# An attention and mixture-of-experts block on one core: another order of the opening, and the weight maxima one step later

## What is computed

```
mod = silu(c) @ wmod                       # sa, ca, ga, sb, cb, gb for each batch
ga, gb = sign(g) * max(|g|, 0.25)
h  = layernorm(x) * (1 + ca) + sa
q, k, v = h @ qkv_w.T + qkv_b;  q, k = relu(.) + 1e-6
num = q . cumsum(k v);  den = max(q . cumsum(k), 1e-6)
x  = x + ga * ((num / den) @ out_w.T + out_b)
h  = layernorm(x) * (1 + cb) + sb
u  = rmsnorm(h @ W_in.T);  top 2 of (u @ Wr.T + bias), softmax over the two
out = sum over the two of gate * rmsnorm((silu(u Wg_e) * (u Wu_e)) @ Wd_e)
x  = x + gb * rmsnorm(out) @ W_out.T
```

## Time and profile before

| | |
|---|---|
| timed runs | 417.27, 417.74, 418.27 us |
| profiled execution | 417.46 us, of which the span is 415.5 us |
| busy share of the span | PE 85%, PEld 74%, DVE 77%, ACT 70%, POOL 59% |
| mean granted clock of PE | 0.944 of full |

### The profile page before, as it was taken

The page is one execution under the profiler, slowest core; times in us unless marked ns, Lnnn a source line. Parts: engine busy times, 40 slices in busy tenths (PEclk is TensorE's granted clock), DMA queues, the critical chain, the costliest instruction groups (busy, mean ns, idle before and its releaser), DMA issues.

```text
span 415.5 us, 12907 instructions
## 1 busy us (share of the span) xinstructions
PE 353.6 (85%) x3750; PEld 308.6 (74%) x3751; DVE 321.0 (77%) x1029; ACT 292.0 (70%) x814; POOL 245.1 (59%) x221
## 2 busy tenths in 40 slices
PE   3799999999999999984049999999999999990464
PEld 2588887888888888873039989889899999980343
DVE  4078898899999999885828878787787778780686
ACT  4344769888888888744617778778778787873595
POOL 1957566788888888865541554554545455463341
PEclk9999999999999999995559999999999999997698
DMA  7997000000000000011412323233232232213833
GB/s 237 399 361 293 4 6 21 27 29 27 25 25 25 25 25 25 28 52 36 144 38 48 66 66 69 65 69 70 57 70 64 64 71 56 65 34 101 350 98 95
DMA packets 46563, 35.68 MB, mean 86 GB/s; under 512 B 36291, under 2 KB 42070, under 8 KB 45750
## 3 DMA queue, kind: packets, MB, share of 16 engines
q1 hardware_dynamic: 41718, 21.21, 18.4%
q0 software_dynamic: 4544, 9.39, 7.0%
q10 hardware_dynamic: 272, 4.72, 3.0%
HBM read 18.69 MB, written 13.47 MB: 77 GB/s over the span
## 4 chain that ended last, share of the span: by engine, by line
PE 52%; DVE 20%; issue 9%; DMA 8%; ACT 7%; POOL 2%; DVEq 1%; SPq 0%; ACTq 0%; POOLq 0%
PE bank L1712 9%; PE bank L1713 8%; PE bank L1714 8%; PE bank L1465 5%; DVE prod L953 4%; PE bank L1727 4%; PE bank L1729 4%; PE bank L1728 4%; DMA gates_bc<-gate_rows 4%; ACT junk L846 2%; PE bank L1543 2%; DVE st L877 1%; DVE rows L1014 1%; DVE wmaxs L1049 1%; DMA dispatched<-rows,pos 1%
## 5 line engine op out<-in xcount | busy, mean ns | idle before, releaser
L570 POOL DMA_INDIRECT expert_rows<-late,to_place x78 | 81.8, 1049 | 82.9 <-DVE late L1326 70.3
L1712 PE MATMUL bank<-late,w_hi 128*128 128x256 f16 x312 | 86.3, 277 | 14.8 <-DMA late<-dispatched 13.4
L1714 PE MATMUL bank<-late,w_lo 128*128 128x256 f16 x312 | 86.2, 276 | 0.0
L1713 PE MATMUL bank<-late,w_hi 128*128 128x256 f16 x312 | 86.2, 276 | 0.0
L1312 DVE SCALAR_TENSOR_TENSOR kv<-bank,uscale,kv 128x512 f32<-128x512 f32 x78 | 58.5, 750 | 32.1 <-ACT kv L788 18.6
L547 POOL DMA_INDIRECT dispatched<-rows,pos x64 | 67.3, 1051 | 26.7 <-issue 18.4
L529 POOL TENSOR_TENSOR kv<-kv,v 128x1024 f32<-128x1024 f32 x32 | 67.6, 2134 | 16.2 <-ACT kv L691 16.2
L1465 PE MATMUL bank<-cst,kv 128*128 128x128 f32 x576 | 74.6, 281 | 1.1 <-POOL kv L529 0.9
L1465 PEld LDWEIGHTS bank<-cst,kv 128*128 128x128 f32 x576 | 69.4, 195 | 1.8 <-POOL kv L529 1.0
L788 ACT ACTIVATE kv<-bank,descale 128x512 f32<-128x512 f32 x78 | 53.6, 687 | 23.3 <-PE bank L1714 19.3
L794 ACT ACTIVATE kv<-kv 128x512 f16<-128x512 f32 x78 | 48.8, 625 | 16.9 <-DVE kv L1312 11.4
(11 more groups left out here) (231 smaller groups left out, 737.4 us busy)
## 6 DMA issues: line engine op xcount, KB each, us to landing
late<-wguT ACTq DMA_DIRECT2D x1, 4096.0 KB, 16.0
late<-expert_rows SPq DMA_DIRECT2D x1, 2064.0 KB, 11.0
gates_bc<-gate_rows SPq DMA_DIRECT2D x1, 2048.0 KB, 15.7
wd<-wdT SPq DMA_DIRECT2D x1, 2048.0 KB, 24.4
out<-kv SPq DMA_DIRECT2D x16, 128.0 KB, 1.8
late<-dispatched SPq DMA_TRANSPOSE x78
expert_rows<-late,to_place POOLq DMA_INDIRECT x78
late<-expert_rows SPq DMA_DIRECT2D x1, 1032.0 KB, 6.6
```

The lines of the kernel that those rows point to most:

```text
L570: pool.indirect_dma_start(ybuf, bass.IndirectOffsetOnAxis(ap=to_place[:, s, r:r + 1], axis=0), yt[:, s, r, :], None).then_inc(y_scat[s], 16)
L1712: mm(o, w_hi[:, w], hi, start=True, stop=False)
L1713: mm(o, w_hi[:, w], lo, start=False, stop=False)
L1714: last = mm(o, w_lo[:, w], hi, start=False, stop=True)
```

## The change

- PE runs seven bf16 matmuls (128x128 by 128x512, on a tile that POOL sets to zero) before anything else, into a bank that is used later.
- Constants have a semaphore of their own, `cst_ld`; waits that need only these name it. The output bias counts with x of batches 2 to 5.
- `wgu` is issued by SP behind `gates_bc`, not by ACT.
- The bias matmuls of batch 0 come ahead of PE's wait for hT.
- The k and v bias is split on DVE, in eight instructions, at the end of its opening; POOL's eleven go.
- The norm of batch 1: square root, reciprocal and shift are done with batch 0's, and ACT's two `xn` instructions right after hT of batch 0.
- POOL's parts of the output bias and its wait for `gates_in` come after the products of batch 1; the four gate products in steps 2 to 5, not 1 to 4. ACT's three casts for the output bias move to step 3.
- The maxima are in steps 3 to 6, and the matmuls that turn and spread them use the second third's bank, so three state matmuls go ahead of them; `weight_power` follows the first products.

```diff
+        warm = prod[:, 1, 0:2 * D].bitcast(BF16)
...
-        MAX_STEPS = range(SCALE_STEP - 5, SCALE_STEP - 1)
-        MAX_ROW = CUM[0][0:1, THIRD * P:THIRD * P + P]
-        MAX_ALL = CUM[0][:, THIRD * P:THIRD * P + 1]
+        MAX_STEPS = range(SCALE_STEP - 4, SCALE_STEP)
+        MAX_ROW = CUM[1][0:1, THIRD * P:THIRD * P + P]
+        MAX_ALL = CUM[1][:, THIRD * P:THIRD * P + 1]
...
-            sp.dma_start(cst[:], consts).then_inc(w_ld, 16)
+            sp.dma_start(cst[:], consts).then_inc(cst_ld, 16)
             sp.dma_start(small[:], weights_all).then_inc(w_ld, 16)
-            sp.dma_start(bo[:], out_b.to_broadcast([P, D])).then_inc(bkv_ld, 16)
+            sp.dma_start(bo[:], out_b.to_broadcast([P, D])).then_inc(x_mid, 16)
...
             sp.dma_start(gates_bc[:], gbuf.to_broadcast([P, B * 2 * D])).then_inc(gates_in, 16)
+            sp.dma_start(wgu, wguT).then_inc(wgu_ld, 16)
             sp.dma_start(xs[:, X_MID * NT:, :], xv[:, X_MID * NT:, :]).then_inc(x_rest, 16)
...
+            nc.gpsimd.memset(warm, 0.0).then_inc(eps_set, 1)
...
-                    if isinstance(b, int) and b == 0:
+                    if isinstance(b, int) and b == 1:
                         out_bias_parts()
-                    if isinstance(b, int) and b < WO_CHUNKS:
-                        if b == 0:
-                            pool.wait_ge(gates_in, 16)
-                        n = B // WO_CHUNKS
-                        ga = gates_bc[:].rearrange("p (b g d) -> p b g d", g=2, d=D)[:, b * n:(b + 1) * n, 0, :]
+                        pool.wait_ge(w_ld, 16)
+                        pool.wait_ge(gates_in, 16)
+                    if isinstance(b, int) and 1 <= b <= WO_CHUNKS:
+                        n, c = B // WO_CHUNKS, b - 1
+                        ga = gates_bc[:].rearrange("p (b g d) -> p b g d", g=2, d=D)[:, c * n:(c + 1) * n, 0, :]
...
                     if isinstance(b, int) and b == 0:
-                        act.dma_start(wgu, wguT).then_inc(wgu_ld, 16)
+                        norm(1, 1, rs, nmr, xn, ln_nm, xn_done)
...
+            norm_inv(1, sd, rs, ln_sd, ln_rs, 1)
+            norm_shift(1, mv, rs, nmr, ln_rs, ln_nm, 1)
...
+            dve.wait_ge(bkv_ld, 16)
+            for i in range(3):
+                nc.vector.tensor_copy(bkv_part[:, i], (bkv_rest if i else bkv[:])).then_inc(bias_part, 1)
+                dve.wait_ge(bias_part, 2 * i + 1)
+                if i < 2:
+                    nc.vector.tensor_tensor(bkv_rest, (bkv_rest if i else bkv[:]), bkv_part[:, i],
+                                            ALU.subtract).then_inc(bias_part, 1)
+                    dve.wait_ge(bias_part, 2 * i + 2)
+            nc.vector.tensor_scalar(bkv3[:], bkv_part[:, 0], ident[0:3, 0:1], None, ALU.mult).then_inc(bias_part, 1)
+            for i in range(1, 3):
+                dve.wait_ge(bias_part, 5 + i)
+                nc.vector.scalar_tensor_tensor(bkv3[:], bkv_part[:, i], ident[0:3, i:i + 1], bkv3[:], ALU.mult,
+                                               ALU.add).then_inc(bias_part, 1)
...
                 if att is not None:
+                    running_products(att, 0)
                     if scale:
                         weight_power(att)
-                    running_products(att, 0)
...
+            pe.wait_ge(eps_set, 1)
+            for _ in range(7):
+                mm(KV[:], warm[:, 0:P], warm, start=True, stop=True)
             pe.wait_ge(sc_done, 1)
...
-                pe.wait_ge(hT_done, b + 1)
                     if first(b):
-                        pe.wait_ge(bkv_ld, 32)
+                        pe.wait_ge(bkv_ld, 16)
                         for t in range(NT):
                             mm(KV[:, t * 2 * D:(t + 1) * 2 * D], ones[0:1, :], bkv[0:1, :], start=(t == 0), stop=False)
+                        pe.wait_ge(hT_done, 1)
+                        pe.wait_ge(w_ld, 16)
```

More of the change, by code:

```diff
@@ L291, in block_kernel @@
         eps_set, x_mid = sem("eps_set"), sem("x_mid")
+        cst_ld = sem("cst_ld")
         sc_done, modcol_ps, modcol_done = sem("sc_done"), sem("modcol_ps"), sem("modcol_done")
@@ L486, in _ @@
             nc.gpsimd.memset(eps_rms[:], RMS_EPS).then_inc(eps_set, 1)
[L487 to L502, removed]
             def out_bias_parts():
                 pool.wait_ge(gate_done, 1)
+                pool.wait_ge(x_mid, 32)
                 nc.gpsimd.tensor_tensor(bo_ga[:], bo[0:B, :], gate_row[:, 0:D], ALU.mult).then_inc(bo_part, 1)
@@ L605, in _ @@
             nc.scalar.activation(sc[:], cT_sb, ACT.Silu).then_inc(sc_done, 1)
-            act.wait_ge(eps_set, 1)
+            act.wait_ge(eps_set, 2)
             nc.scalar.activation(junk[:, 0:1], eps_ln[:], ACT.Sqrt)
@@ L662, in step @@
                     spread(*prj)
[L663 to L667, removed]
+                if nrm is not None and not (isinstance(nrm[0], int) and nrm[0] == 1):
+                    for b, p, n in (nrm, (1, 1, 1)) if isinstance(nrm[0], int) and nrm[0] == 0 else (nrm,):
+                        act.wait_ge(ln_mv, b + 1)
+                        nc.scalar.activation(sd[:, p, :], mv[:, p, :, 1], ACT.Sqrt,
+                                             bias=eps_ln[:]).then_inc(ln_sd, 1)
                 if qkv is not None:
@@ L676, in step @@
                     if isinstance(b, int) and b == 0:
-                        act.dma_start(wgu, wguT).then_inc(wgu_ld, 16)
+                        norm(1, 1, rs, nmr, xn, ln_nm, xn_done)
+                    if isinstance(b, int) and b == 2:
+                        act.wait_ge(bo_part, 6)
+                        for i in range(3):
+                            nc.scalar.activation(bo_ga3[32 * i:32 * i + B, :], bo_ga_part[:, i],
+                                                 ACT.Copy).then_inc(bo_done, 1)
                 if inp is not None:
@@ L700, in step @@
                     nc.scalar.activation(qT[:, p, :], q_raw[:], ACT.Identity, bias=eps_f[:]).then_inc(q_done, 1)
-                if nrm is not None:
+                if nrm is not None and not (isinstance(nrm[0], int) and nrm[0] == 1):
                     norm(nrm[0], nrm[1], rs, nmr, xn, ln_nm, xn_done)
[L703 to L708, removed]
                 if nrm is not None and not isinstance(nrm[0], int):
@@ L923, in _ @@
                                            ALU.add, ALU.mult).then_inc(gate_done, 1)
-            dve.wait_ge(w_ld, 32)
+            dve.wait_ge(w_ld, 16)
+            dve.wait_ge(cst_ld, 16)
             nc.vector.tensor_scalar(wrn[:], wr, innorm, None, ALU.mult).then_inc(w_small, 1)
@@ L1065, in weight_power @@
             def weight_power(att):
-                dve.wait_ge(cum_ps[0][0], att[0] + 1)
+                dve.wait_ge(cum_ps[0][1], att[0] + 1)
                 then(nc.vector.tensor_reduce(wmax_row[:], MAX_ROW, AX.X, ALU.max))
@@ L1073, in weight_scale @@
             def weight_scale(att):
-                dve.wait_ge(cum_ps[1][0], att[0] + 1)
+                dve.wait_ge(cum_ps[1][1], att[0] + 1)
                 then(nc.vector.tensor_copy(wpow[:], MAX_ALL))
@@ L1102, in step @@
                     if isinstance(nb, int) and nb >= 2:
-                        dve.wait_ge(x_mid if nb < X_MID else x_rest, 16 if nb < X_MID else 48)
+                        dve.wait_ge(x_mid if nb < X_MID else x_rest, 32 if nb < X_MID else 48)
                     if not isinstance(nb, int) or nb >= 2:
@@ L1130, in step @@
                     best(rb, rp)
-                if nrm is not None and not (isinstance(nb, int) and nb == 0):
+                if nrm is not None and not (isinstance(nb, int) and nb < 2):
                     norm_inv(nb, sd, rs, ln_sd, ln_rs, np_)
@@ L1443, in running_state @@
                 b, p, n = att
-                if not scale and 0 in chunks:
+                if 0 in chunks:
                     pe.wait_ge(kv_done[t], b + 1)
@@ L1452, in running_state @@
                         pe.wait_ge(gate_done, 1)
-                    if scale and cc == 0:
+                    if scale and cc == 1:
                         if t == 0:
@@ L1459, in running_state @@
                             mm(MAX_ALL, ones[0:1, :], wpow_row[:], start=True, stop=True)
-                        pe.wait_ge(kv_done[t], b + 1)
                     if t == 0 and cc == 2 and not first(b):
@@ L1513, in step @@
                     else:
-                        pe.wait_ge(w_ld, 32)
+                        pe.wait_ge(cst_ld, 16)
                     for t in range(NT):
```

3 lines of the change are left out of this document (2 added, 1 removed).

## The result

| | before | after |
|---|---|---|
| median of 20 runs | 417.64 us (416.61 to 421.95) | 415.09 us (413.71 to 417.89) |
| ratio | | 0.9919, 95% interval 0.9898 to 0.9939 |
| profiled execution, span | 417.46, 415.5 | 414.08, 412.2 |

The changed kernel is faster, by 2.6 us in the medians and 3.4 by the ratio. Forecast were 416.6 us and a gain of 1.1; the time is inside the range of 413.6 to 418.5. The profiled execution did not go the forecast way: it showed the sign and the price of rival A, a fast PE at 15 us.

What follows compares the result with a forecast made beforehand. The opening was taken to wait on the gate-row broadcast and POOL's order behind it, later steps on DVE. Opening gain 3.4 less maxima loss 2.3 made -1.1, so 416.4 us profiled, 416.6 against the median; range 413.6 to 418.5.

Steps and rivals of the forecast that it cites:

- rival A: Opening: warm-ups keep PE's clock up, matmuls fast at 15.2 us, step 3 gains 5.9, total 414.0 us; chance 0.20.
- (a): Start of PE: seven warm-up matmuls delay the modulation matmuls, cost 0.3 us, bounds 0.3 to 1.5.
- (b): Opening: batch 1's norm moved ahead; xn by about 9.6 us, hidden; gate row and DMAs 0.5 to 0.6 later.
- (c): Opening: constants apart from weights; batch 0's transposes at 7.4 us, not 8.46; k and v matmuls 1.7 earlier if slow.
- (d): Opening: bias on DVE takes 3.2 us; batch 1's bias matmul at 15.2 to 15.5, not 18.13; gain 2.8.
- (e): Step 3: gates_in wait behind batch 1's products; PE starts at 26.3 us, not 30.03; gain 3.4 at DVE's first product.
- (f): Opening loads: gates_bc first, wgu lands at about 28 us, hidden with 3 to 6 to spare; cost 0.
- Rival B: Opening loads: gates_bc takes 15.7 us even alone, wgu lands at 37 to 38, total 418.9 us; chance 0.08.
- (g): Maxima moved to steps 3 to 6: step 5 saves 0.5 us, later steps lose 2.8; net loss 2.3.

Runs made afterwards that it cites:

- no_warm: The changed kernel without the seven warm-up matmuls on PE: 415.41 us, ratio 0.9925 to the kernel before.
- after_again: The changed kernel unchanged, run and profiled a second time: 415.15 us, ratio 0.9927 to the kernel before.
- pool_gates_first: The changed kernel with POOL's old order, output bias parts and gates_in wait ahead of batch 1's products: 414.64 us, ratio 0.9909.
- maxima_2_to_5: The changed kernel with the maxima back in steps 2 to 5: 419.58 us, ratio 1.0015 to the kernel before.
- before_pad: The kernel before with eight small memsets added in DVE's opening: 434.87 us, on a chip where the kernel before took 435.97.
- warm_apart: The changed kernel plus spare matmuls in PE's opening gaps, POOL's first products held until DVE's bias ends: 430.07 us, ratio 0.9881 to the kernel before.
- warm_apart_fill: warm_apart plus eight spare matmuls ahead of PE's wait for wmax in step 7: 429.29 us, ratio 0.9881 to the kernel before.

## Why the prediction held, and where it didn't

The time fell in the range, the gain was 2 to 3 times the forecast one. By the steps:

- **(a) Warm-ups.** Cost forecast 0.3, measured 0.25 (4.25 against 4.00), or 0.14 against no_warm (4.11). The clock can come up behind them (after_again), but it fell in the next gap. That was the one before 7.67, not the one between 11 and 15.2 of which the prediction speaks. no_warm shows no loss in time. The cost was right.
- **(b) Norm of batch 1.** xn of batch 1 was there at 9.90 for 9.6, gates_bc issued at 11.10 for 11.4. Hidden, as said.
- **(c), (d) Opening.** Batch 0's transposes started at 7.80 and 7.67, not 7.4: they still waited for the constants, which took 5.6 and 5.4 us from issue to landing and not 4.5. It cost nothing further on. Bias 3.1 us for 3.2; L1551 at 15.74 and, in after_again, 15.54 for 15.2 to 15.5. The size was right for a slow PE: den of step 3 at 26.72 for 26.3, first product at 27.91 for 27.6, step 4 3.5 us early for 3.4. No run takes (b), (c) or (d) out alone, so their shares of the gain are read from the timelines, not shown one by one.
- **(e) POOL's order.** I put the end of the wait down to the move on POOL. pool_gates_first shows that the order of the loads is enough for it: gates_bc in 6.9 us instead of 15.7, and no wait in POOL's old order. Whether the move alone would have been enough too was not tried. The size was right, the cause half wrong.
- **(f) Loads.** Hidden, as said; wgu at 29.3 for 28, 2.7 us to spare where 3 to 6 were forecast. The sum behind the 28 gives 26.4 (11.4 + 15), so the transfer took 2.9 us more than the rate of 426 GB/s has it. maxima_2_to_5 shows the cover from the other side: without the move of the maxima DVE stands 7.36 us. Rival B was wrong: gates_bc alone is not slow. (Its 418.9 also leaves out the 0.28 between profile and median.)
- **(g) Scale step.** The closing 0.60 and 0.59 for 0.5, the maxima exposed 2.79 and 2.81 for 2.84 by the milestones, and at step 8 in after_again 2.77 for 2.8. Net 2.2 for 2.3. Right, but for the dip, which the prediction had at nothing: where PE's clock falls after its wait, 1.2 us more.
- **The step that failed**, though the time fell in the range, is the choice between the forecast and rival A. Its sign, L1554 of batch 1 in 1.1 us, is in the first profile (1.13), and its gain at step 3 of 5.9 was 5.91 (31.05 to 25.14). I took the clock at 15 us to be one thing or the other and gave the slow one the greater chance. It is neither: both came, in the same program. The times of the kernel before scatter too (416.61 to 421.95), but its one trace can't say whether by the clock. Of the changed kernel's two profiles, one had each. Rival A's cause, a clock that is up from the warm-ups on, did not come: in the fast one L1437, at 4.25, and all of batch 0 ran slow, and the matmuls sped up between 13.5 and 14.6 us, after PE had worked on batch 0 from 7.80 with no gap to speak of. Why is open, since in after_again and no_warm PE worked as densely from 7.67 and 7.42 to 13 us and was slow at 14. That the 5.9 came out so well is in part luck.
- **Not in the sum:** 0.34 us in step 8, as the table shows, and 0.1 in every second later step of the loop; by the last den of the phase (184.82 before, 181.19 and 182.81 after) it is 0.7 in both profiles. In the kernel before DVE stood there ahead of L981:

```profile
88.19 0.09 DVE L981 MATCH_VALUE_LOAD i<-m,score 128x8 f32 x1 [0.41 <-DVE m L974]
```

In after the same instruction follows its maximum by 0.33 us in all, start to start, instead of 0.71. No edit is near it. That it is the place of the code in memory is a guess; before_pad, where the stand is gone, speaks for it, but it stays open.

By its own terms the slow case (after_again) gained 2.0 to 2.3 us, the forecast 1.1 and these 0.7 and small change; the fast case gained 3.3 to 3.5.

## What to carry to other kernels

Where transfers share full queues, send first the one whose reader blocks others, and ask what then arrives late: here the late one was paid for by moving its readers a step, where no wait hid them. When PE's work in a stretch may run at either clock, one profile is one draw; compare milestones of several, and put the two cases in the forecast with their chances. An engine that gets faster moves others in time: look for what DVE and POOL will then do side by side.

## What the runs showed of the hardware

- bf16 instructions of 3x256 on DVE took 0.28 and 0.47 us alone, and 2.03 and 2.24 beside POOL's products of 2.1 us; the f32 ones before POOL started kept their 0.41.
- A wait of 1.85 us on PE, in work that is dense otherwise, was enough for its clock to fall to 1.2 GHz in three of six profiled executions and not in the others.
- PE without gaps did not always come up to 2.4 GHz: in warm_apart it worked from 4.25 to 16.3 us and still took 0.64 us for two transposes that take 0.41 at the high rate. The granted clock read 1.00 over the whole stretch.
- The chip of warm_apart ran the kernel before 4% slower. Of that, 3 us fell in the loop's first pass (step 8: 13.46 us in warm_apart_fill, 10.55 in after). ACT stands there for 1.76 us ahead of hT, though PE had made its input (the transposes at 80.08, 0.38 us) by 80.5; the profile puts the wait down to "remote", none of the core's engines. What it is, is open:

```profile
82.32 0.56 ACT L664 ACTIVATE hT<-bank,mod_cols 128x256 f32<-128x256 f32 x1 [1.76 <-remote]
```
